# Softmax sums of a four-layer cross-attention kernel: one fp32 product becomes two fp16 terms, made on ScalarE and GpSimd, and moves behind the second block of scores

## The reference

```python
q, k, v = x @ Wq, ctx @ Wk, ctx @ Wv            # split into heads
logits = einsum('bhqd,bhkd->bhqk', q, k) * scale + col_bias
probs  = softmax(logits, axis=-1)               # exp / sum over 1024 keys
out    = einsum('bhqk,bhkd->bhqd', probs, v)
x      = out @ Wo + bo + x
```

## Time and profile before

| what | value |
|---|---|
| median of 3 runs | 3688.02 us (3687.46 to 3688.6) |
| the profiled execution, its own time | 3687.8 us |
| its span, first to last instruction | 3686.0 us |
| TensorE busy | 96% |
| VectorE, GpSimd, ScalarE busy | 65%, 54%, 46% |
| mean granted TensorE clock | 0.989 of full |

### The profile page before, as it was taken

How to read it: one execution, slowest core, us unless ns; L and a number is a source line. 1 busy time by engine, 2 the same in 40 slices (tenths; PEclk the granted TensorE clock), 3 DMA queues, 4 the chain that set the end, 5 groups by cost and what they waited for, 6 DMA issues and landing times.

```text
span 3686.0 us, 69837 instructions
## 1 busy us (share of the span) xinstructions
PE 3531.1 (96%) x27496; PEld 1554.9 (42%) x27496; DVE 2406.0 (65%) x4483; ACT 1696.2 (46%) x2148; POOL 1995.9 (54%) x964
## 2 busy tenths in 40 slices
PE   6999999999987988989999999999999999999997
PEld 2444444444432222224444444444444444444443
DVE  6666666666666788866666666666566666666663
ACT  4444444444445666664444444444444444444443
POOL 5765666666641000036566666666776666656666
PEclk8999999999998999999999999999999999999998
DMA  4000000000000000000000000000000000000000
GB/s 137 10 10 10 1 10 10 10 1 8 8 4 8 1 8 9 8 2 10 10 1 10 10 10 1 10 10 10 1 10 10 1 10 10 10 1 10 3 1 24
DMA packets 47504, 39.45 MB, mean 11 GB/s; under 512 B 2768, under 2 KB 40784, under 8 KB 47184
## 3 DMA queue, kind: packets, MB, share of 16 engines
q1 hardware_dynamic: 47184, 34.99, 3.0%
HBM read 32.88 MB, written 2.10 MB: 9 GB/s over the span
## 4 chain that ended last, share of the span: by engine, by line
PE 90%; DVE 4%; issue 3%; ACT 2%; POOL 1%; DMA 0%; POOLq 0%; ACTq 0%; DVEq 0%
PE ps_j L663 39%; PE ps_j L815 18%; PE ps_st L767 13%; PE ps_sm L738 7%; PE ps_st L773 3%; PE ps_j L802 3%; PE ps_j L828 2%; PE ps_st L738 1%; PE ps_sm L789 1%; PE ps_j L747 1%; ACT pt L1072 1%; DVE nmg L1367 1%; ACT k_l L1032 1%; DVE k_h L1285 1%; DVE ps_sm L1377 0%
## 5 line engine op out<-in xcount | busy, mean ns | idle before, releaser
L555 POOL TENSOR_TENSOR acc<-acc,pt 128x1024 f32<-128x1024 f32 x576 | 1378.9, 2394 | 258.9 <-ACT pt L1072 217.9
L1072 ACT ACTIVATE pt<-ps_st 128x1024 f32<-128x1024 f32 x768 | 742.9, 1019 | 379.2 <-PE ps_st L773 379.1
L569 POOL TENSOR_TENSOR o_un<-o_un,rinv 128x512 f32<-128x512 f32 x112 | 141.9, 1267 | 1198.4 <-DVE rinv L1410 1198.4
L1377 DVE CUSTOM_DVE_ANT_0 ps_sm<-ps_sm,bias_m,nmx 128x512 f32<-128x512 f32 x760 | 543.5, 756 | 316.9 <-PE ps_sm L738 310.7
L815 PE MATMUL ps_j<-pt,v 128*64 128x512 f32 x3072 | 706.1, 602 | 3.0 <-ACT pt L1072 2.0
L1377 DVE CUSTOM_DVE_ANT_0 ps_sm<-ps_sm,bias_m 128x512 f32<-128x512 f32 x760 | 512.1, 716 | 196.9 <-PE ps_sm L738 194.0
L663 PE MATMUL ps_j<-w_h,ctx_h 128*128 128x128 f16 x3072 | 535.9, 221 | 0.5 <-DVE x L1418 0.5
L663 PE MATMUL ps_j<-w_l,ctx_h 128*128 128x128 f16 x3072 | 533.8, 220 | 0.0
L663 PE MATMUL ps_j<-w_h,ctx_l 128*128 128x128 f16 x3072 | 533.7, 220 | 0.0
L1410 DVE RECIPROCAL rinv<-rinv 128x256 f32<-128x256 f32 x224 | 391.2, 1748 | 73.4 <-ACT rinv L1077 73.4
L663 PE MATMUL ps_j<-ctx_h,w_h 128*128 128x512 f16 x896 | 342.6, 382 | 36.8 <-DVE k_h L1285 13.9
(11 more groups left out here) (139 smaller groups left out, 4791.4 us busy)
## 6 DMA issues: line engine op xcount, KB each, us to landing
w_raw<-wk SPq DMA_DIRECT2D x28, 256.0 KB, 2.8
pt<-ctx_t SPq DMA_DIRECT2D x6, 1024.0 KB, 7.7
w_raw<-wv SPq DMA_DIRECT2D x24, 256.0 KB, 3.6
wo_raw<-wo SPq DMA_DIRECT2D x28, 128.0 KB, 2.0
w_raw<-wq SPq DMA_DIRECT2D x24, 128.0 KB, 2.9
x<-x_t SPq DMA_DIRECT2D x4, 512.0 KB, 8.4
acc<-ctx_t SPq DMA_DIRECT2D x2, 1024.0 KB, 8.3
out_t<-x SPq DMA_DIRECT2D x4, 512.0 KB, 2.7
```

Of the source, the lines that this page charges most:

```text
L555: G.tensor_tensor(total, first, pt[:, n % RING, :], ALU.add).then_inc(s_acc, 1)
L569: G.tensor_tensor(o, o, rinv[:], ALU.mult).then_inc(s_o, 1)
L1072: A(pt[:, n % RING, :], src.rearrange("p h q -> p (h q)"), ACT.Exp).then_inc(s_exp, 1)
L1377: last = V.tensor_tensor_reduce(out=src[:, h, :], in0=src[:, h, :], in1=bias_m[:, t, half * HALF:(half + 1) * HALF], scale=-1.0, scalar=nm ...
```

## The change

In 93 of the 96 wide items (all but 29, 30 and 31, `split_sums`) the total in `acc` is split into two fp16 terms. ScalarE writes `acc_h`, the rounded total (`sums_hi`, behind the first two exponentials of the next slot); GpSimd writes `acc_l`, the rest (`sums_lo`, ahead of its first `add` in that slot). TensorE multiplies both by an fp16 matrix of ones: four fp16 matmuls, two for each half of the result rows. In all items `sums` moves behind score block 1. The orders of the other engines follow: VectorE's two reciprocals stand together, GpSimd does `add(s, 2)` ahead of `normalize`, and ScalarE has `sums_out` behind exponentials 2 and 3 and `keys_hi(s+2, 1)` ahead of `output_hi`. The two terms lie in `sq`; what else used `sq` early on moves to `y_rms` and `v_rms`. The mean-square matrix becomes ones, with the factor 1/C put in the square (`scale=C ** -0.5`).

```diff
             then("pvb", s - 1)
-            then("sum", s - 1)
             then("k0", s + 2)
             bias(0, 0)
             bias(0, 1)
+            if past:
+                then("sum", s - 1)
...
+            def sums_lo(p):
+                pool.wait_ge(s_acc_h, splits(p) + 1)
+                G.tensor_tensor(acc_l, acc[:, p % 2, :], acc_h, ALU.subtract).then_inc(s_acc_l, 1)
...
+                if past and split_sums(s - 1):
+                    sums_lo(s - 1)
                 if summing:
                     add(s, 1)
+                    add(s, 2)
                 if s == G0 + 1:
                     normed_lo(rms_batch(s))
                 if past:
                     normalize(s - 1)
-                if summing:
-                    add(s, 2)
-                if past:
                     output_lo(s - 1)
...
+                if split_sums(p):
+                    pe.wait_ge(s_acc_l, splits(p) + 1)
+                    dst = take("sum", p)
+                    for part in (acc_h, acc_l):
+                        for h in range(2):
+                            last = MM(dst[h * HD:(h + 1) * HD, :], ones_h[:], part[:, h * TQ:(h + 1) * TQ],
+                                      start=part is acc_h, stop=part is acc_l)
+                    last.then_inc(s_sum, 1)
+                    return
...
-                if past:
-                    sums(s - 1)
                 if far:
                     project_k(s + 2, 0)
                 score_block(1)
+                if past:
+                    sums(s - 1)
...
+            def sums_hi(p):
+                act.wait_ge(s_acc, ADDS * (wides(p) + 1))
+                reaches(act, s_sum, p)
+                if p == G1:
+                    act.wait_ge(s_xs, 2 * B)
+                A(acc_h, acc[:, p % 2, :], ACT.Copy).then_inc(s_acc_h, 1)
...
-                if past:
-                    sums_out(s - 1)
+                if past and split_sums(s - 1):
+                    sums_hi(s - 1)
...
                 bias(0, 1)
+                if past:
+                    sums_out(s - 1)
                 if nxt and has_values(s + 1):
                     values(s + 1, 0)
+                if far:
+                    keys_hi(s + 2, 1)
                 if past:
                     output_hi(s - 1)
                 if far:
-                    keys_hi(s + 2, 1)
```

More of the change, by code:

```diff
@@ L157, in passes, with split_sums, splits @@
     return places
+def split_sums(p):
+    return not grouped(p) and not G0 - 3 <= p < G0
+def splits(p):
+    return wides(p) - min(max(p - (G0 - 3), 0), 3)
 def added(kt):
@@ L182, in bank_users @@
                 then("pvb", s - 1, 1)
-                then("sum", s - 1, 1)
                 then("k0", s + 2, 1)
             else:
-                if past:
-                    if not grouped(s - 1):
-                        then("pvb", s - 1)
-                    then("sum", s - 1)
+                if past and not grouped(s - 1):
+                    then("pvb", s - 1)
                 if far:
@@ L308, in build @@
         ident = sb("ident_sb", [P, P], F16)
-        ones = sb("ones_sb", [P, HD], F32)
-        mean = sb("mean_sb", [P, P], F32)
+        ones = sb("ones_sb", [P, P], F32)
+        ones_h = sb("ones_h_sb", [P, HD], F16)
         bias_q = sb("bias_q", [P, TQ], F16)
@@ L327, in build @@
         mask_t = sq[:, 0, :]
-        own_t = sq[:].rearrange("p c t -> p (c t)").bitcast(F16)[:, 0:TK]
-        other_t = sq[:].rearrange("p c t -> p (c t)").bitcast(F16)[:, TK:2 * TK]
+        own_t = y_rms[:].bitcast(F16)
+        other_t = v_rms[:].bitcast(F16)
+        halves = sq[:].rearrange("p c t -> p (c t)").bitcast(F16)
+        acc_h, acc_l = halves[:, 0:2 * TQ], halves[:, 2 * TQ:4 * TQ]
         ps_st = ctx.enter_context(nc.psum_tensor("ps_st", [P, 2, 2, TQ], F32))
@@ L372, in build @@
         s_o_un = sem("s_o_un")
+        s_acc_h = sem("s_acc_h")
+        s_acc_l = sem("s_acc_l")
         s_sum = sem("s_sum")
@@ L827, in sums @@
                 for h in range(2):
-                    last = MM(dst[h * HD:(h + 1) * HD, :], ones[:], acc[:, p % 2, h * TQ:(h + 1) * TQ], start=True,
+                    last = MM(dst[h * HD:(h + 1) * HD, :], ones[:, 0:HD], acc[:, p % 2, h * TQ:(h + 1) * TQ], start=True,
                               stop=True)
@@ L835, in mean_squares @@
                 for c in range(CQ):
-                    last = MM(dst, mean[:], sq[:, c, :], start=c == 0, stop=c == CQ - 1)
+                    last = MM(dst, ones[:], sq[:, c, :], start=c == 0, stop=c == CQ - 1)
                 last.then_inc(s_ms, 1)
@@ L1108, in squares @@
                 act.wait_ge(s_x, 2 * (G0 - B + b) + 2)
+                act.wait_ge(s_sum, G0 - 3)
                 reaches(act, s_xs, B * GROUPED + b)
-                A(sq[:], of_batch(x32, b), ACT.Square).then_inc(s_sq, 1)
+                A(sq[:], of_batch(x32, b), ACT.Square, scale=C ** -0.5).then_inc(s_sq, 1)
             def root_mean_squares(b):
@@ L1432, in _ @@
             V.memset(ones[:], 1.0)
-            V.memset(mean[:], 1.0 / C)
+            V.memset(ones_h[:], 1.0)
             context_lo(0)
@@ L1467, in wide_slot @@
                     normed(rms_batch(s))
-                elif past:
-                    reciprocal(s - 1, 0)
                 peak()
@@ L1477, in wide_slot @@
                 peak()
-                if rms_batch(s) is not None:
+                if past:
                     reciprocal(s - 1, 0)
-                if past:
                     reciprocal(s - 1, 1)
```

## The result

The changed kernel takes **3670.23 us** (median of 5 runs, 3668.35 to 3670.39), the kernel before 3688.6 beside it (5 runs, 3687.46 to 3692.18): a ratio of 0.9947 (0.9933 to 0.9962), 18 us less. The forecast was 3656, 32 less, so a little over half of the gain came. The profiled span is 3666.6 us, the mean granted clock 0.987.

The account below looks back on a forecast made before the run. TensorE, busy 96% of the span, was taken to bound the kernel. From 3687.8 us: 38 less for split items, 11 more for new-layer slots, 4 less around layer 1, 1 less for bank waits: 3656, range 3645 to 3672.

Parts of the forecast that it names:

- common slot: TensorE in each ordinary slot: sums and `attend` cost 0.65 us instead of 1.06, 0.41 less for each of 93 items.
- a closing chain that comes late: Sums to output product: a small lateness, under 0.2 us or so, would leave 3656 to 3672 us; chance 8%.
- the case given 62%: The sum of all terms as it stands, 3650 to 3662 us.
- slots 1, 49, 78, 80, 81, over a common slot: New-layer slots: TensorE waits for GpSimd's late subtraction, four at 2.5 us and one at 0.9, 11 us more.
- around layer 1: Slots 30 and 31: TensorE's wait for VectorE in score block 2 shrinks, 2 us each, 4 less together.
- two bank waits: Two slots in which the key projection waited some 0.6 us for the bank: 1 us less.
- slot 110 to the end: Last items: the split's bare steps are paid back by a shorter chain in item 109's slot; zero, give or take 2.
- The spare times: In a common slot, the subtraction ends 3.8 us before the sums, and the closing chain 0.7 before the output product.
- Rival (d): New-layer slots: waits longer than priced, as GpSimd's delay also moves the adds; 10 us more, 3666; chance 10%.
- rival (c): Closing chain late in each common slot: at 1.5 us later, TensorE waits 0.8 in 88 slots, 3726; chance 4%.
- (a): TensorE's sums: the fp16 halves do not run side by side, a pair costs 0.42 us, 3695; chance 4%.
- (b): TensorE's sums: the weight loads lie bare, 0.14 us lost in each item, 3707; chance 2%.

Follow-up runs that it names:

- the first experiment: The changed kernel with GpSimd's subtraction put first in its slot, ahead of `split_x`, and `add_bo` behind `output_lo`: 3655.74 us, ratio 0.9908.
- the last experiment: The first experiment's kernel with the last three items' sums in fp32 and, in the last two slots, at the old place: 3650.24 us, ratio 0.9893.

## Why the prediction was right, and by how much not

The sign, the mechanism and the common slot were right, and the time lay inside the range. The size was off by 14 us (12 in the profiled execution, 3668.35), most of it in the small terms. That the range held it owes something to luck: it reached to 3672 for a closing chain that comes late, which it does not (0.72 to spare), while the case given 62%, 3650 to 3662, did not come. Each term of the sum beside what the two traces show:

| term | forecast | shown |
|---|---|---|
| common slot, for each split item | -0.41 | -0.385 |
| slots 1, 49, 78, 80, 81, over a common slot | +11 | +15.8 |
| around layer 1 | -4 | -2.9 |
| two bank waits | -1 | -1.2 |
| slot 110 to the end | 0 | +3.55 |

- **Common slot.** `attend` costs 0.11 more, as forecast; the sums 0.56 instead of 0.54. Over the 90 items ahead of slot 110 that is 2 us less gain. Shown by the rows, and the price of a pair by the run with one term.
- **The spare times**, 3.8 and 0.7, were right to 0.05. That the second was needed is shown by the run with the add between.
- **Slots with a new layer.** Here 4.8 us are missing. "I price 4 at 2.5" had the wait right (2.32, 2.42 and 2.44 in slots 1, 80 and 81) and missed what comes behind it: half the clock for some 3 us. Slot 81 lost 3.80 over a common slot (34.73 against 30.93), of which 2.50 is the later start, 0.44 the slower sums and 0.87 the slower projection. Slots 1 and 80 lost 3.94 and 4.07. Rival (d), 3666, put such an excess on delayed adds; the excess was there, for another cause. The cut wait shows the cause: in slot 1 the extra went with the half clock.
- **Slot 78** I had taken for an ordinary one of these. It has two causes. The bias of the last layer's first keys is worked out there, and with the sums gone from their old place the value projection waits for ScalarE to read it (0.63 with no split at all, 1.08 with the subtraction first). The slot was 37.20 before and 37.97 in both these kernels, where 0.385 less was due for the split: 1.2. The late subtraction adds 2.0 (39.98): a wait of 1.59 at the sums, in part in place of that for the bias, and half the clock behind it. Together 3.2, of the 15.8. Why ScalarE reads that bank so late was not followed further.
- **Around layer 1**: slot 30 became 2.04 shorter, as the forecast 2 (39.51 to 37.47), but the stretch from slot 31 to slot 48 only 0.84 (616.20 to 615.36), where I had put another 2. The 2.29 of the earlier trace rows is slot 30's; in slot 31 TensorE waited 1.89 at that place. It waits 0.87 there now, but a new wait of 1.27 for the low half of the queries (`q_l`) follows, so the waits of over 0.4 us in that slot add up to 4.1, and to 4.2 before. Behind the 1.89 the clock fell (a mean of 0.60 over the next 2.5 us), and behind the 0.87 it did not, so even the 0.84 is not all the new order's.
- **The end** failed by as much as the slots with a new layer. It cost 3.55 instead of nothing, and the 38 of the sum had already counted 0.41 for each of the three items whose sums fall there: 4.8 in all. TensorE's waits there, in the changed kernel:

```profile
3605.11 0.61 PE L680 MATMUL ps_j<-o_h,wo_h 128*128 128x512 f16 x1 [1.46 <-POOL o_l L591]
...
3632.85 0.61 PE L680 MATMUL ps_j<-o_h,wo_h 128*128 128x512 f16 x1 [5.33 <-POOL o_l L591]
...
3651.97 0.62 PE L847 MATMUL ps_j<-sq,ones_h_sb 128*64 128x512 f16 x4 [1.94 <-POOL sq L572]
3659.92 0.61 PE L680 MATMUL ps_j<-o_h,wo_h 128*128 128x512 f16 x1 [7.33 <-POOL o_l L591]
```

"A shorter chain pays it back in the slot of item 109" failed: there is less work ahead of the product in the last slots, so a chain that starts 5 us later is late by 5.33 (in the kernel before by 3.29 at the same place), and the very last subtraction costs 1.94 bare. The last row, 7.33, is the same in the kernel before. The run with no split shares the 3.55 out: fp32 sums at the new place cost 1.9 (75.3 against 73.4), and the split the other 1.6; a fall of the clock more or less in these slots is of that size too. With the old place and fp32 for the last items the stretch is 3.7 us shorter than before. That run keeps the other engines' new orders, and what they give there was not tried alone.

The slower side, rival (c), exists and starts where I put it: one add in the wrong place brings it. (a) and (b) are refuted by the run with one term.

The account closes: 90 split items ahead of slot 110 give -34.7, and -34.7 + 15.8 - 2.9 - 1.2 + 3.55 = -19.4, which is what lies between the two spans (3686.0 and 3666.6).

## What to carry to other kernels

Where one engine is at its limit, a helper's new instruction is free only in the slots in which the helper idles: list the slots that carry extra pieces, and put the new instruction ahead of these pieces, not behind. Here that took the kernel from 3670 to 3656 us, after 18 us from the change itself (with `add_bo` moved as well, and 1.6 of it from a clock that held in slot 48, for no reason shown). When you price a wait on TensorE, allow for half the clock behind it, and look at the last slots apart, since a chain that is hidden everywhere else lies bare there.

## What was not expected of the hardware

- A wait of 2.44 us in a stream that had run at a granted clock of 1.00 was followed by 0.50 for about 3 us, and cost 1.3 us beyond itself. After waits of 0.76, 0.79 and 1.39 us it stayed at 1.00; after one of 1.59 it fell, and around the 1.46 at 3605.11, in the last slots, too: the steps behind it were 0.40 instead of 0.22.
- The length of the wait alone does not decide it. In the kernel before, the clock stayed at 1.00 after the 2.29 us in slot 30, and the three matmuls right after a wait of 3.29 in slot 111 still started 0.22 apart; it fell 1 us later. The same wait at the same place went both ways: 1.67 to 1.68 us at the head of slot 48 was followed by a fall in the kernel before, the changed kernel and the run with half of `add_bo` moved, and by none in the first experiment, the run with one term and the last one. The 1.92 us in slot 28 did so too. So one execution of a kernel tells little of the half clock's price; what decides was not tried.
- Two fp16 matmuls on the two halves of the result rows start within 0.03 us of each other (two are recorded in 0.41, one in 0.38) and together cost 0.216 us, the step of one.
- The profiles of three kernels (no split, the add between, the last experiment) reach the last scores of block 0 in their first slot at 75.3 to 75.4 us, those of the kernel before, the changed kernel and the first experiment at 71.0 to 71.6. Nothing in the changes explains it. The three profiled executions (3698.41, 3752.21 and 3651.45 us) are the slowest or the second slowest of their kernels, so it may belong to the execution; it stays open.
